# Turning half of the attention exponentials by VectorE blocks and DRAM instead of by TensorE, in a decoder layer on one core

## The reference

```python
def attention(q, k, v, mask):
    scores = jnp.einsum('bhqd,bhkd->bhqk', q, k) / jnp.sqrt(jnp.float32(HD))
    scores = scores * mask - 10000.0 * (1.0 - mask)
    probs = jax.nn.softmax(scores, axis=-1)
    return jnp.einsum('bhqk,bhkd->bhqd', probs, v)
ln_out = layernorm(hidden_states, ln1_s, ln1_b)
q, k, v = jnp.split(ln_out @ w_qkv + b_qkv, 3, axis=-1)
x = hidden_states + attention(heads(q), heads(k), heads(v), ltor_mask) @ w_ao + b_ao
...
x = x + attention(heads(q), heads(k), heads(v), cross_mask) @ w_co + b_co
return x + gelu(layernorm(x, ln3_s, ln3_b) @ w1 + b1) @ w2 + b2
```

## Time and profile before

| | |
|---|---|
| Median of 3 runs | 2041.2 us (2039.52 to 2042.16) |
| Span of the profiled execution | 2038.2 us, 3.0 under the median |
| TensorE busy | 2018.1 us, 99% |
| VectorE busy | 1447.7 us, 71% |
| ScalarE busy | 1166.7 us, 57% |
| DMA | 190.25 MB in 332469 packets, the hardware queue's packets 32.5% of the 16 engines' span |

### The profile page before, as it was taken

The page is one execution under the profiler, slowest core; times in us unless marked ns, Lnnn a source line. Parts: engine busy times, 40 slices in busy tenths (PEclk is TensorE's granted clock), DMA queues, the critical chain, the costliest instruction groups (busy, mean ns, idle before and its releaser), DMA issues. The chain is left out here.

```text
span 2038.2 us, 41730 instructions
## 1 busy us (share of the span) xinstructions
PE 2018.1 (99%) x14096; PEld 1621.0 (80%) x14096; DVE 1447.7 (71%) x3874; ACT 1166.7 (57%) x3239; POOL 450.6 (22%) x434
## 2 busy tenths in 40 slices
PE   9999999999999999999999999999999999999998
PEld 8877777777777777777777776788888888888887
DVE  7798988888889888888888898565344443435333
ACT  4388888888888888787788888522111121212111
POOL 1011111111113242222232233053031331313000
PEclk9999999999999999999999999999999999999999
DMA  8513243243144344344334334432212212121201
GB/s 270 171 35 77 83 119 77 64 113 97 48 141 133 109 134 109 85 121 126 86 111 123 95 108 120 138 99 70 80 33 77 46 62 72 41 77 46 64 24 47
DMA packets 332469, 190.25 MB, mean 93 GB/s; under 512 B 210688, under 2 KB 276864, under 8 KB 332288
## 3 DMA queue, kind: packets, MB, share of 16 engines
q1 hardware_dynamic: 332288, 187.97, 32.5%
HBM read 137.00 MB, written 50.86 MB: 92 GB/s over the span
## 5 line engine op out<-in xcount | busy, mean ns | idle before, releaser
L1279 ACT ACTIVATE A_p<-A_p,A_nmax 128x256 f32<-128x256 f32 x1024 | 509.1, 506 | 0.0
L1564 DVE TENSOR_TENSOR A_p<-A_sc,A_mk 128x1024 f32<-128x1024 f32 x256 | 312.7, 1221 | 109.1 <-PE A_tp L1046 108.9
L1574 DVE CUSTOM_DVE_ANT_0 A_p<-A_p,A_ma 128x256 f32<-128x256 f32 x1024 | 374.5, 423 | 5.2
L1285 ACT ACTIVATE A_pt<-A_tp 128x512 f32<-128x512 f32 x512 | 276.9, 592 | 142.2 <-PE A_tp L1046 141.8
L1046 PEld LDWEIGHTS A_tp<-A_ident,A_p 128*128 128x128 f32 x2048 | 230.1, 141 | 71.8 <-issue 44.1
L1046 PE MATMUL A_tp<-A_ident,A_p 128*128 128x128 f32 x2048 | 274.2, 277 | 2.0 <-ACT A_pt L1285 1.6
L1279 ACT ACTIVATION_READ_ACCUMULATOR A_p<-A_p,A_nmax 128x1 f32 x1024 | 202.8, 198 | 0.0
L1414 ACT ACTIVATE A_mk<-A_tp,A_cols 128x512 f32<-128x512 f32 x62 | 42.7, 689 | 269.0 <-PE A_tp L68 269.0
L766 POOL TENSOR_TENSOR A_res<-A_res,A_o_bias 128x512 f32<-128x512 f32 x64 | 84.9, 1338 | 473.1 <-DVE A_nmax L1574 281.3
L1414 ACT ACTIVATE A_ma<-A_tp,A_cols 128x512 f32<-128x512 f32 x62 | 42.8, 690 | 242.4 <-PE A_tp L68 242.4
L66 PE MATMUL A_banks<-A_xt_h,A_w_h 128*128 128x512 f32 x384 | 161.3, 420 | 0.9 <-DVE A_res L1543 0.5
(11 more groups left out here) (245 smaller groups left out, 4856.4 us busy)
## 6 DMA issues: line engine op xcount, KB each, us to landing
A_x<-x SPq DMA_DIRECT2D x96, 256.0 KB, 3.6
A_res<-x SPq DMA_DIRECT2D x64, 256.0 KB, 2.9
A_rt<-inverses SPq DMA_DIRECT2D x512, 32.0 KB, 1.8
x<-A_res SPq DMA_DIRECT2D x64, 256.0 KB, 3.2
turned<-A_x SPq DMA_DIRECT2D x240, 64.0 KB, 2.3
inverses<-A_turned_inv SPq DMA_DIRECT2D x512, 1.0 KB
A_e<-ctx_t SPq DMA_DIRECT2D x16, 512.0 KB, 3.9
A_xt_l<-turned SPq DMA_DIRECT2D x16, 512.0 KB, 4.0
```

Source lines behind the costliest of these rows:

```text
L1279: act.activation(p[:, g % 2, j, t, :], p[:, g % 2, j, t, :], ACT.Exp, scale=-1.0, bias=nmax[:, g % 2, j, t:t + 1], accum_out=rsum[:, g % 2 ...
L1285: act.activation(pt[:, j, :, :], tp[:, j % 2, :].rearrange("p (c s) -> p c s", c=TPB), ACT.Copy)\
L1564: dve.tensor_tensor(p[:, g % 2, heads, :, :].rearrange("p j t s -> p j (t s)"), sc[:, heads, :], m, ALU.mult)\
L1574: dve.tensor_tensor_reduce(out=a_, in0=a_, in1=ma[:, b, t, :], scale=-1.0, scalar=BIG, op0=ALU.add, op1=ALU.min, accum_out=nmax[:, g % 2, ...
```

## The change

Of the four heads of a group, heads 0 and 1 (`MOVED` = 2) are no longer turned by TensorE. VectorE turns their exponentials in place, in blocks of 32x32, with one instruction over 128 x 1024 elements. SyncE stores them to a DRAM tensor with four DMAs, one for each 32 partitions, in pieces of 32 elements (128 bytes), each at the place where its block belongs; there a row of one key holds 128 queries. One DMA loads them into `pt` in pieces of 512 bytes. `pt` holds these two heads in another order, which `turned_keys` picks. Heads 2 and 3 (`TURNS` = 2) are still turned by TensorE, both at the start of the slot. ScalarE takes the exponentials of heads 0 and 1 first in the slot. The masking of heads 0 and 1 now waits for the stores instead of for the turn. The block transpose stands on VectorE behind `scaled` and ahead of the maxima; the loads stand first in SyncE's slot, the stores between the stores and the loads of the inverse sums.

```diff
+MOVED = 2
+TURNS = HPG - MOVED
...
+            def store_exponentials(r, h):
+                grp, _, g = group(r, h, 0)
+                sp.wait_ge(p_blk, grp + 1)
+                wait(sp, ld_p, (grp - 1) * DMA)
+                keys = p_dram[g % 2].rearrange("j t (b i) q -> i (j t b) q", i=32)
+                for n in range(P // 32):
+                    rows_ = slice(n * 32, (n + 1) * 32)
+                    own = p[rows_, g % 2, 0:MOVED, :, :].rearrange("i j t (b q) -> i (j t b) q", q=32)
+                    sp.dma_start(keys[:, :, rows_], own).then_inc(st_p, DMA)
+            def load_exponentials(r, h, pv):
+                grp, _, g = group(r, h, -1)
+                if grp == 0:
+                    sp.wait_ge(w_lo, 3 * KT)
+                else:
+                    sp.wait_ge(done, pv[1])
+                sp.wait_ge(st_p, (grp + 1) * (P // 32) * DMA)
+                sp.dma_start(pt[:, 0:MOVED, :, :].rearrange("p j a (b q) -> p (j a b) q", q=P),
+                             p_dram[g % 2].rearrange("j t (c p) q -> p (j t c) q", p=P)).then_inc(ld_p, DMA)
...
             def slot(r, k, h, a_, b_, own, pv):
                 if own:
+                    load_exponentials(r, h, pv)
                     store_inverses(r, h)
...
+                if exists(k, h, 0):
+                    store_exponentials(r, h)
+                if own:
                     load_inverses(r, h)
...
-            def turn(r, k, h, j):
+            def turn(r, k, h, i):
                 grp, _, g = group(r, h, -1)
+                n, j = grp * TURNS + i, MOVED + i
                 pe.wait_ge(exped, grp * HPG * TPB + (j + 1) * TPB)
-                wait(pe, pt_ok, grp * HPG + (j - 1))
+                wait(pe, pt_ok, n - 1)
...
             def weigh(r, h, bank):
-                pe.wait_ge(pt_ok, (grp + 1) * HPG)
+                pe.wait_ge(pt_ok, (grp + 1) * TURNS)
+                pe.wait_ge(ld_p, (grp + 1) * DMA)
...
                 if own:
-                    turn(r, k, h, 2)
-                    turn(r, k, h, 3)
+                    for i in range(2, TURNS):
+                        turn(r, k, h, i)
...
+                first = TPB * MOVED
+                if now:
+                    for n in range(first):
+                        exponential(r, h, n)
                 if own:
-                    for j in range(HPG if bare else 2):
-                        turned_out(r, h, j)
-                if now:
-                    exponential(r, h, 0)
-                    exponential(r, h, 1)
+                    for i in range(TURNS if bare else 2):
+                        turned_out(r, h, i)
...
             def mask_scores(r, k, h, part):
-                wait(dve, turned, (grp - 2) * HPG + 2 * (part + 1))
+                if heads.start < MOVED:
+                    wait(dve, st_p, (grp - 1) * (P // 32) * DMA)
+                if heads.stop > MOVED:
+                    wait(dve, turned, (grp - 2) * TURNS + heads.stop - MOVED)
...
+            def exponentials_in_blocks(r, h):
+                grp, _, g = group(r, h, 0)
+                dve.wait_ge(exped, grp * HPG * TPB + MOVED * TPB)
+                own = p[:, g % 2, 0:MOVED, :, :].rearrange("p j t s -> p (j t s)")
+                dve.transpose(own, own).then_inc(p_blk, 1)
...
                 if leaves and not late(k, h):
                     scaled(r, h, pv)
+                if exists(k, h, 0):
+                    exponentials_in_blocks(r, h)
                 if coming:
                     maxima(r, k, h, 0)
...
+    exponentials = nc.dram_tensor("exponentials", [2, MOVED, TPB, S, P], F32, kind="Internal").ap()
```

More of the change, by code:

```diff
@@ L1033, in scores @@
                 last.then_inc(scored, 1)
-            def turn(r, k, h, j):
+            def turn(r, k, h, i):
                 grp, _, g = group(r, h, -1)
-                if NG * k + h - LAG - 1 == 0 and j == 0:
+                n, j = grp * TURNS + i, MOVED + i
+                if grp == 0 and i == 0:
                     pe.wait_ge(pgt_ok, B)
@@ L1040, in turn, with turned_keys @@
                 pe.wait_ge(exped, grp * HPG * TPB + (j + 1) * TPB)
-                wait(pe, pt_ok, grp * HPG + (j - 1))
-                if j < 2 and h in (0, 7) and k == (h == 0):
-                    pe.wait_ge(x_lo, (r + (h == 7)) * TT + (j + (3 if h == 0 else 1)))
+                wait(pe, pt_ok, n - 1)
+                if i < 2 and h in (0, 7) and k == (h == 0):
+                    pe.wait_ge(x_lo, (r + (h == 7)) * TT + (n % 2 + (3 if h == 0 else 1)))
                 for t in range(TPB):
                     for c in range(TPB):
-                        last = pe.transpose(tp[:, j % 2, c * S + t * P:c * S + (t + 1) * P],
+                        last = pe.transpose(tp[:, n % 2, c * S + t * P:c * S + (t + 1) * P],
                                             p[:, g % 2, j, t, c * P:(c + 1) * P], ident[:, :])
                 last.then_inc(turned, 1)
+            def turned_keys(j, c):
+                return pt[:, j, :, c * P:(c + 1) * P] if j < MOVED else pt[:, j, c, :]
             def weigh(r, h, bank):
@@ L1118, in slot @@
                 if even is not None:
-                    pe.wait_ge(pt_ok, group(r, h, -1)[0] * HPG + 4)
+                    pe.wait_ge(pt_ok, (group(r, h, -1)[0] + 1) * TURNS)
                     turn_rows(r + (k < NU), even, tp[:, 0, :])
@@ L1153, in hidden @@
                 elif first and f < EARLY:
-                    pe.wait_ge(pt_ok, GROUPS * HPG)
+                    pe.wait_ge(pt_ok, GROUPS * TURNS)
                 else:
@@ L1280, in exponential, with turned_out @@
                                bias=nmax[:, g % 2, j, t:t + 1], accum_out=rsum[:, g % 2, t, j:j + 1]).then_inc(exped, 1)
-            def turned_out(r, h, j):
+            def turned_out(r, h, i):
                 grp, _, g = group(r, h, -1)
-                act.wait_ge(turned, grp * HPG + (j + 1))
-                act.activation(pt[:, j, :, :], tp[:, j % 2, :].rearrange("p (c s) -> p c s", c=TPB), ACT.Copy)\
+                n = grp * TURNS + i
+                act.wait_ge(turned, n + 1)
+                act.activation(pt[:, MOVED + i, :, :], tp[:, n % 2, :].rearrange("p (c s) -> p c s", c=TPB), ACT.Copy)\
                     .then_inc(pt_ok, 1)
@@ L1346, in slot @@
                 bare = k == NU and h < 2
+                first = TPB * MOVED
+                if now:
+                    for n in range(first):
+                        exponential(r, h, n)
                 if own:
-                    for j in range(HPG if bare else 2):
-                        turned_out(r, h, j)
-                if now:
-                    exponential(r, h, 0)
-                    exponential(r, h, 1)
+                    for i in range(TURNS if bare else 2):
+                        turned_out(r, h, i)
                 if leaves and not late(k, h):
                     weighed(r, k, h)
+                if now:
+                    exponential(r, h, first)
                 if own and not bare:
[L1356 to L1359, removed]
+                    for i in range(2, TURNS):
+                        turned_out(r, h, i)
                 unit_out(a_, k)
                 if now:
-                    exponential(r, h, 3)
-                    exponential(r, h, 4)
+                    for n in range(first + 1, 5):
+                        exponential(r, h, n)
                 if even is not None:
@@ L1859, in decoder_layer_and_nonlocal @@
     d = {k[len("L0_xattn_"):]: v for k, v in a.items() if k.startswith("L0_xattn_")}
-    whole_network(nc, a["ctx_2048"], {**nl, "pg_t": a["pg_t"], "pg_b": a["pg_b"]}, m1t, inverses, turned, a["x"], x1, x2, a["ctx_t"],
+    whole_network(nc, a["ctx_2048"], {**nl, "pg_t": a["pg_t"], "pg_b": a["pg_b"]}, m1t, inverses, exponentials, turned, a["x"], x1, x2, a["ctx_t"],
                   a["mask_1x1xSxS2_fc1"], a["mask_Bx1xSxS2_ff1"],
```

5 lines of the change are left out of this document (3 added, 2 removed).

## The result

The change makes the kernel slower: 2267.97 us (2265.69 to 2270.42, 4 runs) against 2041.05 (2039.52 to 2042.16), a ratio of 1.111 with an interval of 1.1094 to 1.1125. That is +227 us where the forecast had +99, and 3 us above the top of its range.

What follows compares the result with a forecast made beforehand. It took TensorE to bound the attention slots (9.31 us each), VectorE close behind. With VectorE becoming the bound (+37) and late stores (+62), 2038.2 became 2137.2, plus 3.0 for the runs' median: 2140 us, range 2055 to 2265.

Steps and rivals of the forecast that it cites:

- free in light slots: TensorE needs the loaded exponentials only at the slot's end: issued at 0.5 us, landed by 5, used at 8.3, no cost.
- TensorE's 137 us are not paid out: In the attention slots TensorE falls from 9.31 to 8.24 us, 137 us in all, but VectorE and the stores take over.
- VectorE becomes the bound in light slots, at 9.6 us: Each slot's added block transpose costs 1.20 us, making a block 76.7 us against 74.5; +35 us, carried as +37.
- Piece prices: On the DMA engines a 128-byte piece costs 12 ns and a 512-byte piece 29 ns.
- A store's issue, 0.77 us: SyncE's issue of one exponentials store of 1024 pieces takes 0.77 us, between bounds of 0.51 and 1.02.
- SyncE's circle: Time between SyncE's successive exponentials stores: 6.6 us in light slots, 11.6 in slot 4, 13.0 in slot 5, 9.2 in slot 7.
- Slot 6 regains the slack: After slots 4 and 5 cost 4.4 us per block, slot 6 restores the stores' 1.0 us of slack; +62 us for 14 blocks.
- fits on average: The DMA engines need 8.5 of a slot's 9.6 us, which fits on average, not in slots with more.
- B: Rival: the transport binds in most slots; 2219 us, up to 2265 if tile and new stores fill the engines together; chance 0.22.
- A: Rival: VectorE alone binds while SyncE and the DMA keep up; 2078 us, from 2043 without its small gaps; chance 0.23.
- D: Rival: faster, the block transpose runs at twice the rate, 0.69 us; -30 us, 2011 us; chance 0.04.
- C: Rival: TensorE's clock falls in the new slots, one fall every two slots adding 122 us, 2262 us; chance 0.03.

## Why the prediction was wrong

The forecast was 37 (VectorE) + 62 (stores late behind slots 4 and 5) + 0 (the load) = 99 us. In the same terms, added in this order, the runs gave 23 + 105 + 99 = 227: without transport 2064, with the stores 2169, with the load 2268. So of the 128 us missed, -14 are VectorE's, 43 the stores' and 99 the load's. The load's, which the forecast put at nothing ("free in light slots"), is the step that failed most.

Split further along one path of runs it is 23 (VectorE) + 8 (stores, large) + 97 (128-byte pieces of both kinds, and three more issues per tile) + 99 (the load beside them). On another path, with the load put in ahead of the small pieces, the last two are 43 and 153; the parts are not independent.

- **TensorE's 137 us are not paid out:** right. Its transposes went from 274.2 to 159.8 us and the time didn't fall with them.
- **VectorE becomes the bound in light slots, at 9.6 us:** right in kind, and large by 14 us. The transpose took 1.233 us for 1.20. The blocks of the kernel without transport took 76.1 us in the mean of 12 for the forecast 76.7, but the same blocks had taken 74.7 before, not 74.5. The price was +23 for +37.
- **Piece prices:** right. A 128-byte piece took 12.9 ns in the mean (forecast 12), one of 512 bytes 29.4 (forecast 29). With the forecast 8.5 us of DMA per slot and the 11.1 us that a slot now lasts in the mean, the share would be 0.76; it is 0.78:

```profile
400.00:600.00 200.00, 166.88 (x1317) 123.20 (x1315) 171.35 (x490) 123.92 (x380) 23.84 (x27) 0.97 0.78 174
```

- **A store's issue, 0.77 us:** right in the mean (0.757), but not as it was meant. It has no fixed length. Four take 2.25 us in light slots, under the forecast's 2.8, and 2.9 to 4.6 in the crowded ones.
- **SyncE's circle:** slot 4 right (11.33 for 11.6). Slot 5, mis-sized: 15.84 for 13.0. (The forecast's items add up to 11.5 and 12.7; with the gaps between them in the earlier trace rows the latter is 13.0. Landing less drain is 1.5 us, not 1.6, so the slack was 1.1. Neither matters here.) Of the 2.8 us missing, 0.83 are the two loads of `A_res` ahead of the stores, which the forecast left out; 0.7 are the loads of `A_rt` at 2.48 for 1.8; 0.4 are `x<-A_res` at 1.83 for 1.41; the rest are small gaps and stores. Its effect, with the load away: 15.4 us in the interval 5 to 6, against 9.1 without transport. That is 6.3 of the 7 us per block that the stores cost.
- **"Slot 6 regains the slack": the step that failed, with the next.** In the kernel after, the stores of slot 6 run into the backlog (4.64 us) and the queue needs until slot 3 of the next block to be on time again. Most of the loss still stands in the two heavy intervals: of the 13.3 us per block that VectorE's maskings wait for the stores, 10.8 are in 4 to 5 and 5 to 6 (mean of the 12 blocks).
- **"TensorE needs the loaded half only at the slot's end ... free in light slots": this failed most.** The load was costed at 0.43 us of SyncE and nothing else. It took 99 us, or 43 where the stores and tiles went in large pieces. Without it the queue recovers behind slot 5 within a slot, and TensorE's 87 us of waiting for it are gone. That its 1.85 us of all DMA engines do this, and not TensorE's wait, is the likely reading, and not shown. The forecast took the DMA sum, 8.5 of 9.6 us, as "fits on average", and asked only the issue queue for lateness. At 89% of a slot 1.1 us are left to work off a backlog.

**The rivals.** B (2219, up to 2265) came nearest, and its upper end in part for its reason: the tile stores' small pieces and the new stores' cost 91 us and 74 us when each is taken away, 153 together. But B had the transport bind in most slots, and the maskings waited in 67 of 256 cases; outside 4 to 5 and 5 to 6 only 7 to 0 (0.6 us) and 0 to 1 (1.1) have a wait to speak of. That the number fell near B's is luck in part: B had no price for the load either. A (2078) is about what the transport-free kernel gives (2064), and D fell with the transpose's 1.233 us. C: the forecast's sign of it came: the granted clock is 0.967 in the mean, and fell to 0.50 in the stops behind slot 5, and in some other places, where TensorE had been waiting before (it was busy 2.90 us of the 5 from 639 to 644). The Trainium skill ("TensorE: Matmul & The Clock Gate", Why this matters for your kernels) warns of idle gaps between bursts of matmuls, and the trace agrees. What the clock costs by itself was not tried, but it is hardly on the path: from 104 to 1510 us VectorE waited 206.5 us for the stores and 0.7 for TensorE.

What stays open: how the 91 us of the tile stores divide between their issues and their pieces, and the 99 us of the load between its bytes and TensorE's wait for it.

## What to carry to other kernels

A transfer that is hidden in each light slot can still have a price, because it stands beside the heavy ones and takes the time in which a shared queue recovers from them: cost it in the busiest stretch, and ask how long the backlog lasts behind it. Here, with both the issue queue and the DMA engines near full, moving work to another queue or slot mostly moved the wait (6 us more, 34 less, 4 more); taking pieces or bytes away helped (74, 91 and 99 less). Run the kernel with the transport left out early: it divided 227 us into 23 and 204 at once.

## What the runs showed of the hardware

The time for which SyncE issues a DMA depends on the backlog, not on the count of pieces alone. The view of the line with the stores in the kernel after (min, median, max in ns), then their landing:

```profile
L554 SPq DMA_DIRECT2D exponentials<-A_p x512: 303/571/3406, 104.0 to 1512.3; - x171
...
DMA to landing us min/median/max: 2.1/3.4/5.8
```

With large pieces and no load the same 128 KB took 302/421/1119 ns to issue and landed in a median of 2.2 us. So with a thirty-second of the pieces the median issue is a quarter shorter, while in the kernel after the longest is six times the median. The four that took 4.64 us, from 645.10 on, stand where the DMA share is 0.93.

A DMA issued from ScalarE's stream holds ScalarE in the same way. From the run with stores and load on ScalarE (four store issues, then ScalarE's next instruction):

```profile
635.31 5.15 ACTq L1301 DMA_DIRECT2D exponentials<-A_p  x4
...
640.51 0.60 ACT L1281 ACTIVATE A_v<-A_banks 128x512 f32<-128x512 f32 x1 [5.35 <-issue]
```

A round trip of small transfers is slow beside bulk ones: for the inverse sums VectorE waited at most 2.5 us at a time in the kernel without transport, and up to 7.5 with stores and load on ScalarE in large pieces.
